# Layer 3 attention on one Trainium2 core: keys and queries in two halves of 64 partitions

## The reference, cut to what matters

```python
q = q_input @ W_Q + b_Q
k = kv_input @ W_K + b_K
v = kv_input @ W_V + b_V
q = q.reshape(B, LQ, N_HEAD, D_H).transpose(0, 2, 1, 3)
...
sim = jnp.einsum('bhqd,bhkd->bhqk', q, k) / jnp.sqrt(jnp.float32(D_H))
sim = jnp.where(mask, neg_inf, sim)
attn = jax.nn.softmax(sim, axis=-1)
out = jnp.einsum('bhqk,bhkd->bhqd', attn, v)
out = out.transpose(0, 2, 1, 3).reshape(B, LQ, D_MODEL)
return out @ W_O + b_O
```

## Time and profile before

| | us |
|---|---|
| median of 3 runs | 1753.84 (1751.29 to 1755.04) |
| the profiled execution: its time | 1752.74 |
| its span, first to last instruction | 1751.0 |
| PE busy | 1501.6 (86%) |
| DVE busy | 1248.1 (71%) |
| ACT busy | 838.4 (48%) |
| POOL busy | 329.3 (19%) |

### The profile page before, as it was taken

One profiled execution on the slowest core, in us unless ns is written; L12 is line 12 of the kernel. 1 busy time (PEld: TensorE's weight loads), 2 busy tenths in 40 slices (PEclk: granted clock), 3 DMA queues, 4 the chain that ended last, 5 costly groups with the idle time before them and its releaser, 6 DMA issues. The chain is left out here.

```text
span 1751.0 us, 39790 instructions
## 1 busy us (share of the span) xinstructions
PE 1501.6 (86%) x15246; PEld 1268.9 (72%) x15246; DVE 1248.1 (71%) x2541; ACT 838.4 (48%) x1257; POOL 329.3 (19%) x453
## 2 busy tenths in 40 slices
PE   3897377455899999999999999478999999996995
PEld 2897255345799999999999998235777777774895
DVE  4312653486688888888888885437888888884598
ACT  1332132142566666666666663044666666653432
POOL 0110000001333333334333330012111111100330
PEclk9899687766999999999999999788999999998898
DMA  1111689110111111111111100015654565450110
GB/s 35 49 37 33 154 218 213 30 36 1 50 48 45 37 35 35 35 35 36 57 47 36 35 0 3 4 40 135 144 120 115 126 144 118 118 109 30 45 37 22
DMA packets 93076, 115.83 MB, mean 66 GB/s; under 512 B 12337, under 2 KB 78306, under 8 KB 92962
## 3 DMA queue, kind: packets, MB, share of 16 engines
q1 hardware_dynamic: 92962, 114.19, 26.3%
HBM read 76.35 MB, written 0.46 MB: 44 GB/s over the span
## 5 line engine op out<-in xcount | busy, mean ns | idle before, releaser
L2315 DVE TENSOR_REDUCE l3att_parts<-PS 112x1 f32<-112x500 f32 x384 | 245.7, 669 | 55.5 <-PE PS L2053 48.1
L1732 ACT CAST l2att_PT<-PS 125x512 fp32r<-125x512 f32 x336 | 175.3, 595 | 221.3 <-PE PS L1671 221.3
L1772 DVE TENSOR_REDUCE l2att_neg<-PS 128x1 f32<-128x1500 f32 x112 | 192.7, 1721 | 76.8 <-PE PS L1664 76.8
L1778 DVE TENSOR_TENSOR l2att_PT<-PS,l2att_PT 125x512 fp32r<-125x512 f32 x336 | 210.2, 681 | 1.5 <-ACT l2att_PT L1732 1.5
L2180 ACT ACTIVATE l3att_P<-PS 125x1344 f32<-125x1344 f32 x128 | 165.2, 1291 | 76.9 <-PE PS L2072 76.9
L1671 PEld LDWEIGHTS PS<-all_ident,l_P 128*125 128x125 f32 x1344 | 163.5, 187 | 15.0 <-DVE l_P L1786 6.5
L1741 ACT ACTIVATE l_P<-PS,l2att_neg 128x1500 f32<-128x1500 f32 x112 | 171.0, 1526 | 3.9 <-DVE l2att_neg L1772 3.9
L1703 PE MATMUL PS<-l2att_PT,l_cc 125*128 125x256 f32 x576 | 170.5, 296 | 0.0
L1671 PE MATMUL PS<-all_ident,l_P 128*125 128x128 f32 x1344 | 165.4, 273 | 4.8 <-DVE l_P L1786 4.8
L2053 PE MATMUL PS<-l3att_KS,l3att_QB 97*112 97x500 f32 x384 | 156.6, 462 | 10.6 <-POOL l3att_QB L2240 4.1
L1705 PE MATMUL PS<-l2att_PT,l_cc 125*128 125x256 f32 x576 | 162.5, 282 | 0.0
(11 more groups left out here) (569 smaller groups left out, 2864.3 us busy)
## 6 DMA issues: line engine op xcount, KB each, us to landing
l3att_KS<-l3att_kh SPq DMA_DIRECT2D x128, 187.5 KB, 3.9
l_QP<-in_ctxT SPq DMA_DIRECT2D x8, 1500.0 KB, 12.1
l_cT<-in_ctxT SPq DMA_DIRECT2D x16, 750.0 KB
l_c<-in_ctx SPq DMA_DIRECT2D x16, 750.0 KB
l3att_cT<-in_ctxT SPq DMA_DIRECT2D x16, 750.0 KB, 4.4
l3att_KS<-l3att_kl SPq DMA_DIRECT2D x64, 187.5 KB, 4.7
l_QP<-in_ctx SPq DMA_DIRECT2D x8, 1344.0 KB
l0f_w<-in_L_ffn_W SPq DMA_DIRECT2D x16, 256.0 KB, 3.1
```

The lines of the kernel that those rows point to most:

```text
L1732: act.copy(PT[:, 4 * g:4 * g + 4, PLACE[u1], 0, :], PS[0:CHUNK, 3 * s1 + g, :].rearrange("k (c r) -> k c r", r=128)).then_inc(hi_in, 1)
L1772: v.tensor_reduce(neg[:, s:s + 1], E, XY_AXES, ALU.max, negate=True).then_inc(top_in, 1)
L1778: v.tensor_tensor(PT[:, 4 * g:4 * g + 4, at, 1, :], PS[0:CHUNK, 3 * s1 + g, :].rearrange("k (c r) -> k c r", r=128), PT[:, 4 * g:4 * g + 4 ...
L2315: v.tensor_reduce(parts[:, u % 2, half, i:i + 1], PS[0:HROWS, PLACES[p], 0:BANK_KEYS], X_AXIS, ALU.max, negate=True).then_inc(top_in, 1)
```

## The change

`KS` and `QB` get 115 partitions (`DEEP`) in two parts that begin at partitions 0 and 64 (`STEP`). Each part serves two of the set's four heads, that is one half of 112 queries: 16 rows of high, 16 of low keys at 0, mask row at 32 (`MARK`) and two rows of ones, 16 rows of high keys at 35 (`LOW`), 51 rows in all. The rows between 51 and 64 are ones in `KS` against zeros in `QB`. A maxima's score contracts the 51 rows of its half instead of all 97. The places are renumbered: half `p % 2`, keys `p // 2`, so that (0, 1), (2, 3), (4, 5) are the two halves of the same keys. Place 3 goes ahead of the values' projection. A transposed score contracts 115 rows. `remap` makes 6 x 4 copies of 16 rows and two of the mask, after both `kh` and `kl` are complete. The queries' weights are loaded in pieces of 16 columns, the bias as rows that PE transposes; a sign column, a second product on DVE (`t3`) and an addition on POOL over all partitions replace the low part's subtraction. The mask column of `QB` comes from the bias row instead of from a load of ones.

```diff
         PLACES = (0, 2, 0, 2, 0, 1)
+        WIDTH, STEP = 16, 64
+        MARK, LOW = 32, 35
+        SPAN = LOW + WIDTH
+        DEEP = STEP + SPAN
...
-            QB = [self.sb(ctx, f"QB{s}", [99, SETS, SET_ROWS], F32R) for s in range(2)]
-            KS = [self.sb(ctx, f"KS{s}", [99, SETS, KEYS], F32R) for s in range(2)]
+            QB = [self.sb(ctx, f"QB{s}", [DEEP, SETS, SET_ROWS], F32R) for s in range(2)]
+            KS = [self.sb(ctx, f"KS{s}", [DEEP, SETS, KEYS], F32R) for s in range(2)]
...
-                for r in range(3):
-                    sp.dma_start(WQ3[:, :, r, :], t["L3_xattn_W_Q"].rearrange("i (g r) -> i g r", r=32)
+                sp.wait_ge(empty, 1)
+                for at in (0, WIDTH, LOW):
+                    sp.dma_start(WQ3[:, :, at:at + WIDTH], t["L3_xattn_W_Q"].rearrange("i (x r) -> i x r", r=WIDTH)
                                  ).then_inc(q_w_in, 16)
-                    for g in range(SETS):
-                        sp.dma_start(bq3[32 * r:32 * r + 32, g:g + 1],
-                                     t["L3_xattn_b_Q"][32 * g:32 * g + 32].unsqueeze(1)).then_inc(q_w_in, 16)
+                    sp.dma_start(rowq[:, :, at:at + WIDTH], t["L3_xattn_b_Q"].rearrange(
+                        "(g f r) -> g f r", f=2, r=WIDTH)).then_inc(q_w_in, 16)
...
-                    sp.dma_start(KS[s][96:97, :, :].bitcast(F32),
-                                 maskb[b:b + 1, :].bitcast(F32).unsqueeze(1).to_broadcast([1, SETS, KEYS])
-                                 ).then_inc(mask_in[s], 16)
+                    for f in range(2):
+                        at = STEP * f + MARK
+                        sp.dma_start(KS[s][at:at + 1, :, :].bitcast(F32),
+                                     maskb[b:b + 1, :].bitcast(F32).unsqueeze(1).to_broadcast([1, SETS, KEYS])
+                                     ).then_inc(mask_in[s], 16)
+                    sp.wait_ge(kh_in, BANKS * b + BANKS)
+                    sp.wait_ge(kl_in, BANKS * b + BANKS)
                     for g in range(SETS):
-                        for r, src, done in ((0, kh[s], kh_in), (1, kh[s], kh_in), (2, kl[s], kl_in)):
-                            sp.wait_ge(done, BANKS * b + BANKS)
-                            sp.dma_start(KS[s][32 * r:32 * r + 32, g, :].bitcast(F32),
-                                         src[32 * g:32 * g + 32, :].bitcast(F32)).then_inc(ks_in[s][g], 16)
+                        for f in range(2):
+                            rows = slice(2 * WIDTH * g + WIDTH * f, 2 * WIDTH * g + WIDTH * f + WIDTH)
+                            for at, src in ((0, kh[s]), (WIDTH, kl[s]), (LOW, kh[s])):
+                                sp.dma_start(KS[s][STEP * f + at:STEP * f + at + WIDTH, g, :].bitcast(F32),
+                                             src[rows, :].bitcast(F32)).then_inc(ks_in[s][g], 16)
...
-                            half, i = p // BANKS, p % BANKS
+                            half, i = p % 2, p // 2
...
                             pe.matmul(PS[0:HROWS, PLACES[p], 0:BANK_KEYS],
-                                      QB[s][0:97, g, HROWS * half:HROWS * half + HROWS],
-                                      KS[s][0:97, g, BANK_KEYS * i:BANK_KEYS * i + BANK_KEYS],
+                                      QB[s][STEP * half:STEP * half + SPAN, g, HROWS * half:HROWS * half + HROWS],
+                                      KS[s][STEP * half:STEP * half + SPAN, g, BANK_KEYS * i:BANK_KEYS * i + BANK_KEYS],
                                       start=True, stop=True).then_inc(sr_ps, 1)
...
                     if now:
-                        rows((2,))
+                        rows((2, 3))
                     if late or g >= 2 and more:
...
-                    if now:
-                        rows((3,))
                     if then:
                         turned(0)
...
                 def low_queries(n):
                     g.wait_ge(qh_in, n + 1)
-                    g.tensor_tensor(queries(n)[32:64], wide(t2[n % 2][32:64, :]), queries(n)[32:64], ALU.subtract
-                                    ).then_inc(q3_in, 1)
+                    g.wait_ge(t3_in, n + 1)
+                    g.tensor_tensor(queries(n), wide(t3[n % 2][:, :]), queries(n), ALU.add).then_inc(q3_in, 1)
...
+                    v.wait_ge(t2_in, n + 1)
+                    v.tensor_scalar(t3[n % 2][:, :], t2[n % 2][:, :], lows[:, 0:1], None, ALU.mult
+                                    ).then_inc(t3_in, 1)
```

More of the change, by code:

```diff
@@ L1951, in _ @@
                 for s in range(2):
[L1952 to L1955, removed]
+                    for rows in (slice(MARK + 1, LOW), slice(SPAN, STEP), slice(STEP + MARK + 1, STEP + LOW)):
+                        sp.dma_start(KS[s][rows, :, :].bitcast(F32).rearrange("p g (c k) -> p (g c) k", k=CHUNK),
+                                     one_row(rows.stop - rows.start, SETS * CHUNKS)).then_inc(ones_in, 16)
                 sp.dma_start(cT[1][:, :], t["ctxT"][1]).then_inc(ct_in[1], 16)
@@ L2020, in _ @@
                         pe.wait_ge(t2_in, n - 1)
-                    pe.matmul(PS[0:96, 6 + n % 2, 0:HALF_TOK], WQ3[:, n // 2, :, :].rearrange("p a r -> p (a r)"),
+                    two = n // 2 * 2
+                    pe.matmul(PS[0:DEEP, 6 + n % 2, 0:HALF_TOK],
+                              WQ3[:, two:two + 2, :].rearrange("p f r -> p (f r)")[:, 0:DEEP],
                               tokens(n % 2), start=True, stop=True).then_inc(q_ps, 1)
@@ L2166, in _ @@
                     values_out(act, 0, 0, i, 3 + i)
+                act.wait_ge(sign_in, 1)
                 for n in range(2 * SETS):
                     act.wait_ge(t2_in, n + 1)
-                    act.copy(queries(n), wide(t2[n % 2][:, :])).then_inc(qh_in, 1)
+                    act.activation(queries(n), wide(t2[n % 2][:, :]), ACT.Identity, scale=sign[:, 0:1]
+                                   ).then_inc(qh_in, 1)
                 def one(n, u, known):
@@ L2222, in _ @@
                 chain(g.memset(SEL[:, :, :], 0.0))
-                chain(g.memset(BM[:, :], 1.0))
-                for r in range(3):
-                    rows = BM[32 * r:32 * r + 32, :]
-                    chain(g.affine_select(out=rows, in_=rows, compare_op=ALU.is_ge, fill=0.0, base=0,
-                                          pattern=[[-8, SETS]], channel_multiplier=1))
-                    chain(g.affine_select(out=rows, in_=rows, compare_op=ALU.is_ge, fill=0.0, base=7,
-                                          pattern=[[8, SETS]], channel_multiplier=-1))
                 chain(g.affine_select(out=SEL[:, :, :], in_=SEL[:, :, :], compare_op=ALU.not_equal, fill=1.0,
@@ L2232, in _ @@
                 g.sem_inc(cleared, 1)
+                chain(g.memset(BM[:, :, :], 1.0))
+                for x, (at, size, apart) in enumerate(((LOW, WIDTH // 2, WIDTH // 2), (0, WIDTH // 2, WIDTH // 2),
+                                                       (WIDTH, WIDTH // 2, WIDTH // 2), (MARK, LOW - MARK, 0))):
+                    band = BM[:, x, :].rearrange("p (f h) -> p f h", f=2)
+                    chain(g.affine_select(out=band, in_=band, compare_op=ALU.is_ge, fill=0.0, base=-at,
+                                          pattern=[[-STEP, 2], [-apart, 2]], channel_multiplier=1))
+                    chain(g.affine_select(out=band, in_=band, compare_op=ALU.is_ge, fill=0.0, base=at + size - 1,
+                                          pattern=[[STEP, 2], [apart, 2]], channel_multiplier=-1))
+                g.sem_inc(bands, 1)
+                g.wait_ge(sign_in, 1)
+                for x in range(1, 4):
+                    chain(g.tensor_tensor(BM[:, 0, :], BM[:, 0, :], BM[:, x, :], ALU.add))
                 def low_queries(n):
                     g.wait_ge(qh_in, n + 1)
[L2236 to L2237 removed]
+                    g.wait_ge(t3_in, n + 1)
+                    g.tensor_tensor(queries(n), wide(t3[n % 2][:, :]), queries(n), ALU.add).then_inc(q3_in, 1)
                 def block_queries(b, s, x):
                     g.tensor_tensor(
[L2241 to L2243 removed]
+                        QB[s][:, x, :].rearrange("p (h q) -> p h q", q=TOK),
+                        Q3[:, x, bass.ds(b, 1), :].to_broadcast([DEEP, SETS, TOK]),
+                        BM[:, 0, :].unsqueeze(2).to_broadcast([DEEP, SETS, TOK]), ALU.mult).then_inc(qb_in, 1)
                 for n in range(2 * SETS):
```

46 lines of the change are left out of this document (27 added, 19 removed).

## The result

| | before | after |
|---|---|---|
| median, us | 1754.44 (1751.29 to 1755.79, 4 runs) | **1807.18** (1801.45 to 1810.9, 4 runs) |
| ratio, 95% interval | | **1.030** (1.0268 to 1.0333) |
| the profiled execution: its time, its span | 1752.74, 1751.0 | 1808.85, 1807.1 |

The change costs 3%. The forecast was 1793 with a range of 1767 to 1811: the side is as forecast, the time lies in the range, 14 us above the point.

A forecast was written before the change was run, and what follows sets the result against it. PE's work per group and its order were taken as the bound. Group terms of 0.76, 0.79, 0.84 and 0.25 made 2.64 us a batch, +40.6 in all on 1752.74, giving 1793 us, range 1767 to 1811.

The forecast's parts named there:

- The mechanism: In PE's group: paired halves stream together, saving 0.23 us where both are ready; each height change costs about 0.20.
- an estimate of 1709: Maxima's scores: the skill page's doubled rate alone would halve 384 x 0.23, saving 44 us; the forecast did not adopt it.
- over (0,1): Group's first pair: entry +0.22, pairing saves 0.23, exit to the maxima's transposes +0.13.
- over (2,3) and the projection: Group's second pair: entry +0.24, exit +0.22, staggered pairing saves 0, lost cover of ACT's copy +0.23.
- over (4,5): Group's last pair: entry +0.20, pairing saves 0.23, exit to the value sums already paid.
- lost cover: Before transposed score five: without place 3 there, the wait for ACT's copy of the projection grows by 0.23 us.
- bank 2: At pair (2,3): DVE frees this bank 0.6 us after bank 0, so the pair runs staggered and saves about nothing.
- changeover: PE entering or leaving a pair: 0.20 to 0.24 us each, 0.10 to 0.13 to the transposes; five new per group.
- Rival E: PE's height changes cost half, 0.10 each; about 1.2 us a batch, +18, 1771 us; chance 14%.
- POOL hides both: Stage start: POOL's work covers SP's three loads for the bias rows and two more for ones; 0, within 1 us.
- rival D: Remap comes late: SP's 26 DMAs hold each batch's first scores 1 to 2 us, +15 to +30, 1815; chance 8%.
- mostly without projections: Last batch of the stage: described so, it was put at +1.0 us, beside 39.6 for the other fifteen.

The follow-up runs named there:

- e3: Changed kernel with its maxima's scores contracting all 115 rows, order and loads as changed; 1778.21 us, ratio 1.0148.
- e4: Changed kernel with scores at all 115 rows and place 3 back behind the values' projection; 1763.75 us, ratio 1.0061.
- e1: Kernel before with only place 3 moved ahead of the values' projection, scores at full height; 1773.6 us, ratio 1.0118.
- e7: e4 with the second buffer's three loads of ones issued behind the first batch's copies; 1758.56 us, ratio 0.9999.
- e10: The changed kernel once more, unaltered, for a second profile; 1809.61 us, ratio 1.0312.
- e2: Kernel before with the maxima's scores contracting 64 rows instead of 97, nothing paired; 1803.14 us, one run.
- e5: Changed kernel with place 3 back behind the projection, so places 2 and 3 stand alone at half height; 1799.81 us, ratio 1.025.
- e11: Changed kernel without SP's 24 key copies from the third batch on, so later batches use old keys; 1800.65 us, ratio 1.0247.

## Why the prediction held, and where it was short

**The mechanism held.** PE's order sets the time; two halves stream together (0.48 for both); each change of height opens a weight load. By the runs, of the 2.19 us a batch the order has 1.05 (e3 less e4) and the half height 1.14 (after less e3). The Trainium skill's factor of two (TensorEngine Tiling (Array Packing), Theoretical Speedup), which gave an estimate of 1709, is reached only inside a pair's own stream; the kernel is 98 us away from it.

**The group's terms, one by one**, in the group at 1407.91, against the one of its kind before, at 1403.80, which the forecast put at +0.79:

| from, to | forecast | measured | how |
|---|---|---|---|
| transposed scores to keys, over (0,1) | +0.13 | +0.04 | 1.44 now, 1407.07 to 1408.51; 1.40 before |
| keys to the fifth transposed score, over (2,3) and the projection | +0.69 | +0.66 | 3.45 now, 1408.51 to 1411.96; 2.79 before |
| fifth transposed score to values, over (4,5) | -0.03 | -0.06 | 0.81 now, 1411.96 to 1412.77; 0.87 before |
| sum | +0.79 | +0.64 | |

By the medians of all batches the four kinds of group came to +0.64, +0.65, +0.73 and +0.18, where 0.76, 0.79, 0.84 and 0.25 stood: 2.19 instead of 2.64. e1 put the order's part at 1.07, and its expectation, made after the result with the forecast's lost cover and bank 2, at 1.04. **The term that was too large is thus the changeover.** With the order at 1.04, 1.60 a batch were left for the half height in the forecast; it is 1.14. In the first kind of group five changeovers stood at 0.22, 0.13, 0.24, 0.22 and 0.20, together 1.01. By the medians of the records' starts and ends against e3 they are about 0.19, 0.08, 0.18, 0.20 and 0.19, together 0.84 and 0.17 on average. The small one is the exit to the transposes, whose load is 3 columns wide. Rival E, with 0.10 each and about 1.2 a batch, falls: 2.19 is nearer to the forecast's 2.64. The alternating L909 and L911 gave 0.20 as the upper end, and three of my terms had gone above it.

**The start was put at 0 and is 5.8.** The step "POOL hides both" failed. It counted SP's loads (two more) and not their size: one load of ones for each buffer now covers 13 partitions. Its fallback, "without POOL as cover, SP's loads could cost 2", was too small also. e7 shows the cause for 3.3 of it. POOL as cover failed too: DVE's second products were to run beside ACT's conversions, and POOL's eight low parts wait for them, 1.9 of the other 2.6 us.

**SP's remap cost nothing in the steady part**, as forecast (e4's batch), so rival D falls in the form given to it. But its traffic stood in the forecast only as a possible late landing. The stops, 5.7 us, were in no case of mine.

**The clock was not in the sum**, about 7 us in the profiled execution; another had less (the last groups of e10 are 19.8 us instead of 21.3, the first 30.4 instead of 31.3). The forecast read 1.00 in the steady part and took it for the whole stage, and set the last batch, "mostly without projections", at 1.0 us.

**How it adds up**: forecast of the groups 40.6, steady terms at their measured size 30.7 in 14 batches and 3.1 in the first four and last three groups; clock 7, stops 5.7, start 5.8, ahead of the stage 3.3. Two misses partly cancel: a mechanism sized a fifth too high (40.6 against 33.8), against three terms set at nothing that come to 18 us. That the time fell into the range is owed in part to this, and in part to the range's upper end of 1811, which was set for half of rival D, a late remap that did not come.

**What was said of the changed profile**: batches of 27.7 (27.24); pairs that start together at (0,1) and (4,5), staggered at (2,3) (record 0.75 instead of 0.48); the fifth transposed score waiting 0.4 (0.43 before its load, in the row below, against 0.21 before; the bracket of 0.24 in PE's own row is shorter because the record before it reaches into the wait); PE's loads idle with "issue" at each exit (0.23) but with no such mark before the pairs; DVE waiting above 1.3 before the first reduction (0.83, and again 0.84 before places 4 and 5). The last was simply a wait that I put in one place, and it comes in two.

```profile
1411.96 0.29 PEld L2086 LDWEIGHTS PS<-l3att_QB,l3att_KS 115*125 115x125 f32 x2 [0.43 <-ACT l3att_VS L2163]
```

## What to carry to other kernels

Price a pair of half-height matmuls with its neighbours: here two streams of 500 columns that overlap save 0.23 us, and a pair among full-height work gives back 0.18 to 0.20 at each side (0.08 at the exit to a narrow product), so it pays only where one side is a narrow product already, or in long runs of pairs (L1118). Where a small product moves in a hand-written order, first look at the wait that it covered; here that cost nearly as much per batch as the halves did. And read a load's issue time on its queue, not the number of loads, before it is called hidden.

## What the runs showed of the hardware that I had not expected

- A load's price on SP's queue can fall on the ones behind it. Of the six loads of ones, the two with 13 partitions issue in 0.94 and 1.85 us, the four with 2 partitions in 0.73, 2.09, 3.04 and 2.66. Two of the same 2 partitions took 0.83 and 1.57 in the kernel before, and with three of them put later (e7) the six have these times:

```profile
L1960 SPq DMA_DIRECT2D l3att_KS<-all_ones x6: 712/932/2377, 1176.2 to 1204.1; - x6
```

  The median falls from 1.97 to 0.93 us for the same six loads.
- PE's granted clock differs at the same place between executions of one program: in 1214 to 1219 us it is 0.53 in one profile of the changed kernel and 0.74 in the other (e10).
- PE can stop for 1 to 3 us in a steady loop with no wait that the profile shows (2.81 us in the changed kernel, with the data queue at 92.8% just before, and 1.73 in e10), and its granted clock is lower behind that (0.57 and 0.66). The cause is not shown.
- Half-height scores can go with a long stretch at the lower clock: 0.50 in e2 11 to 16 us into the groups, where the kernel before has 1.00 (1201.5 to 1206.5 us, as far in). Other kernels with half-height scores have it shorter (1.00 at 1214 to 1219 us in e5 and e11).
